# Attention block with a two-expert feed-forward: weighing the values with one 32-bit product per block instead of three 16-bit ones

## The reference, cut to what matters

```python
x = x + _L0_conv_ref(_ln_c(x), qkv_w, rpb, proj_w, proj_b)      # x: (8, 128, 56, 56)
t = _to_tokens(x)
t = t + _L0_ffn_ref(_ln_t(t), W_router, W1, b1, W2, b2)         # top 2 of 8 experts
x = _from_tokens(t, x)

def _L0_conv_ref(x, qkv_w, rpb, proj_w, proj_b):                # 16 heads of 8, window 7x7
    ...
    attn = jax.nn.softmax(logits, axis=-1)                      # over 49 neighbours
    for a in range(KSZ):
        va = jnp.take(v, si + a, axis=2)
        for c in range(KSZ):
            vac = jnp.take(va, sj + c, axis=3)
            out = out + attn[..., t, None] * vac
            t += 1
    y = out @ proj_w.T + proj_b
```

## Time and profile before

| | |
|---|---|
| time, 3 runs | 3146.11, 3155.05, 3156.77 us; median 3155.05 us |
| profiled execution | 3149.2 us, its span 3147.4 us |
| busy in the span | PE 79%, PEld 67%, DVE 75%, ACT 67%, POOL 75% |
| granted TensorE clock, mean | 0.904 |
| `scores` of the first and last unit | 84.5 us and 2264.7 us after the span's start |
| first and last product of the experts | 2366.4 us and 2965.3 us |

### The profile page before, as it was taken

How to read it: one execution, slowest core, us unless ns; L and a number is a source line. 1 busy time by engine, 2 the same in 40 slices (tenths; PEclk the granted TensorE clock), 3 DMA queues, 4 the chain that set the end, 5 groups by cost and what they waited for, 6 DMA issues and landing times. The chain is left out here.

```text
span 3147.4 us, 119476 instructions
## 1 busy us (share of the span) xinstructions
PE 2482.8 (79%) x34587; PEld 2108.7 (67%) x34692; DVE 2353.8 (75%) x12579; ACT 2122.5 (67%) x5724; POOL 2360.1 (75%) x2808
## 2 busy tenths in 40 slices
PE   4788887888788878888888878888709999999633
PEld 2677777777777777777777777777606666666522
DVE  2688887888788878888788878888746666666444
ACT  0677777777677777777777777777726777777400
POOL 2578888888888888888888888888946777777600
PEclk9999999999899999999999989999959999999855
DMA  2566555555555655555565555556455444444499
GB/s 49 145 126 119 121 124 119 114 122 118 112 106 122 123 118 110 118 117 117 114 120 118 118 109 119 121 117 123 92 99 94 93 92 93 93 93 92 98 314 299
DMA packets 743654, 378.47 MB, mean 120 GB/s; under 512 B 414595, under 2 KB 712227, under 8 KB 743078
## 3 DMA queue, kind: packets, MB, share of 16 engines
q1 hardware_dynamic: 690278, 235.46, 39.5%
q10 hardware_dynamic: 24192, 81.67, 9.9%
q0 software_dynamic: 28608, 54.48, 5.7%
HBM read 232.92 MB, written 98.11 MB: 105 GB/s over the span
## 5 line engine op out<-in xcount | busy, mean ns | idle before, releaser
L1004 ACT ACTIVATE pr<-sc,nmx 128x100 f32<-128x100 f32 x3136 | 922.3, 369 | 103.8 <-DVE nmx L670 100.6
L905 POOL TENSOR_TENSOR pl<-pt 100x512 f16<-100x512 f32 x784 | 815.3, 1040 | 217.9 <-ACT pt L1012 217.4
L670 DVE CUSTOM_DVE_ANT_0 sc<-bank,near 128x100 f32<-128x100 f32 x3136 | 632.3, 256 | 182.7 <-PE bank L490 133.4
L1012 ACT ACTIVATE pt<-bank 100x512 f32<-100x512 f32 x784 | 462.5, 590 | 365.9 <-PE bank L516 353.0
L490 PE MATMUL bank<-kimg,qexp 128*128 (+2 forms) x9408 | 651.5, 221 | 55.3 <-issue 40.0
L490 PEld LDWEIGHTS bank<-kimg,qexp 128*128 128x128 bf16 (+1 forms) x9408 | 567.7, 102 | 103.1 <-issue 71.7
L1385 POOL DMA_INDIRECT yrows<-ye,meta x420 | 451.1, 1074 | 188.6 <-issue 127.6
L516 PE MATMUL bank<-vwin,pt 100*128 100x65 bf16 (+1 forms) x6272 | 417.0, 199 | 202.7 <-DVE om L700 142.6
L516 PEld LDWEIGHTS bank<-vwin,pt 100*128 100x128 bf16 x6272 | 371.9, 102 | 277.1 <-issue 184.6
L911 POOL TENSOR_TENSOR oml<-om 128x256 f16<-128x256 f32 x784 | 483.4, 617 | 57.3 <-DVE om L700 35.4
L499 PE MATMUL bank<-cst_sb,pr 128*100 128x128 f32 x3136 | 503.9, 286 | 0.0
(11 more groups left out here) (150 smaller groups left out, 4665.4 us busy)
## 6 DMA issues: line engine op xcount, KB each, us to landing
vwin<-v_pix SPq DMA_DIRECT2D x1120, 60.5 KB
near<-bias_rows ACTq DMA_DIRECT2D x112, 600.0 KB
y<-yrows SPq DMA_DIRECT2D x112, 224.0 KB, 4.8
qexp<-qring SPq DMA_DIRECT2D x896, 14.0 KB
v_pix<-vrow SPq DMA_DIRECT2D x56, 225.8 KB
xin<-in_x SPq DMA_DIRECT2D x56, 224.0 KB
xres<-in_x SPq DMA_DIRECT2D x112, 112.0 KB, 4.6
x<-xres SPq DMA_DIRECT2D x112, 112.0 KB
```

The source lines that it names most:

```text
L670: i = v.tensor_tensor_reduce(out=sc[:, ring(m, par), k, :], in0=ps_s[m % 2][:, k, :], in1=near[:, st, ct, k, :], scale=-1.0, scalar=-MASKE ...
L905: g.tensor_tensor(pl[:, m % 2], pt[:, m % 2], pt_h[:, m % 2], ALU.subtract).then_inc(s["t_out"], 1)
L1004: i = a.activation(pr[:, r, k, :], sc[:, r, k, :], ACT.Exp, bias=nmx[:, r, k:k + 1], scale=-1.0)
L1012: i = a.activation(pt[:, m % 2].rearrange("p a q -> p (a q)"), ps_t[m % 2][0:NKEY, :], ACT.Copy)
```

## The change

The values are stored and loaded as one 32-bit number instead of two 16-bit halves of the same total size, ACT writes them from PSUM alone, and `a_v_l` on DVE is gone. The probabilities are used as they stand in `pt`; `split_t` on POOL and its tile `pl` are gone. `weigh` makes one 32-bit product per block and waits for the eviction (`th_done`). The lags of `weigh` and of all that follows it (`pick`, `split_l`, folding and projecting) become one slot shorter. The lag of the transposes stays.

```diff
-L_T, L_V, L_P, L_H, L_F = 3, 5, 6, 7, 8
+L_T, L_V, L_P, L_H, L_F = 3, 4, 5, 6, 7
...
-        vwin = asb("vwin", [NKEY, 2, NTILE, 2, VW], BF16)
+        vwin = asb("vwin", [NKEY, 2, NTILE, VW])
...
-                    pe.wait_ge(s["t_out"], n + 1)
+                    pe.wait_ge(s["th_done"], n + 1)
...
-                            p_h, p_l = pt_h[:, m % 2, 2 * t + blk, :], pl[:, m % 2, 2 * t + blk, :]
-                            v_h, v_l = (vwin[:, st, 2 * u + t, part, 64 * blk:64 * blk + 65].bitcast(dt)
-                                        for part, dt in enumerate((BF16, FP16)))
-                            for n, (a_, b_) in enumerate(((p_h, v_h), (p_h, v_l), (p_l, v_h))):
-                                mm = pe.matmul(ps_av[m % 2][:, 2 * t + blk, :], a_, b_, start=n == 0, stop=n == 2)
+                            mm = pe.matmul(ps_av[m % 2][:, 2 * t + blk, :], pt[:, m % 2, 2 * t + blk, :],
+                                           vwin[:, st, 2 * u + t, 64 * blk:64 * blk + 65], start=True, stop=True)
...
-                def a_v_l(I):
...
-                LATE_STEPS = {9: a_q_l, 10: a_k_l, 12: a_v_l}
+                LATE_STEPS = {9: a_q_l, 10: a_k_l}
...
-                def split_t(J, m, par):
-
-                    n = UPP * J + m
-                    g.wait_ge(s["th_done"], n + 1)
-                    g.tensor_tensor(pl[:, m % 2], pt[:, m % 2], pt_h[:, m % 2], ALU.subtract).then_inc(s["t_out"], 1)
...
-                        i = a.activation(vrow[:, :, 0, 65 * blk:65 * blk + 64],
+                        i = a.activation(vrow[:, :, 65 * blk:65 * blk + 64],
...
-                    i.then_inc(s["v_h"], 1)
+                    i.then_inc(s["v_out"], 1)
```

More of the change, by code:

```diff
@@ L103, in sem @@
             return ctx.enter_context(nc.semaphore(name))
-        v_pix = nc.dram_tensor("v_pix", (B * IMG, 2, VW), BF16, kind="Internal").ap()
+        v_pix = nc.dram_tensor("v_pix", (B * IMG, VW), FP32, kind="Internal").ap()
         bias_rows = nc.dram_tensor("bias_rows", (3, 128, 3 * 4 * NKEY), FP32, kind="Internal").ap()
@@ L159, in build @@
         pad = asb("pad", [HEADS, PADW, PADW])
-        vrow = asb("vrow", [HALF, NROW, 2, VW], BF16)
+        vrow = asb("vrow", [HALF, NROW, VW])
         sc = asb("sc", [128, RING, 4, NKEY])
@@ L164, in build @@
         pt = asb("pt", [NKEY, 2, 4, 128])
-        pl = asb("pl", [NKEY, 2, 4, 128], FP16)
         rec = asb("rec", [128, 4])
@@ L204, in build @@
         rowsb = rows[:].bitcast(BF16)
-        pt_h = pt[:].bitcast(BF16)[:, :, :, 1::2]
         om_h = om[:].bitcast(BF16)[:, :, :, :, 1::2]
@@ L218, in build @@
         names = """w_in w_scaled w1_in cst_in rpb_in pad_out gath_in turned win_in bias_done zeroed pad_zero
-            x_in mean_done xc_done sq_done v_h sub_done th_done oml_done
+            x_in mean_done xc_done sq_done sub_done th_done oml_done
             var_done ve_done root_done spread_done xn_done q_done q_h q_out k_done k_h k_out v_done v_out v_store q_exp0 q_exp1
-            v_in0 v_in1 s_done max_done exp_done t_done t_out av_done rec_done orec_done om_done
+            v_in0 v_in1 s_done max_done exp_done t_done av_done rec_done orec_done om_done
             o_done o_out proj_done proj_out bias_out near_in0 near_in1 xres_in0 xres_in1 x1_store0 x1_store1
@@ L312, in store_v @@
                     sp.wait_ge(s["v_out"], I + 1)
-                    dst = bass.AP(v_pix.tensor, I * (PAIR * 2 * VW), [[2 * VW, HALF], [HALF * 2 * VW, NROW], [1, 2 * VW]])
-                    sp.dma_start(dst, vrow[:].rearrange("p n a c -> p n (a c)")).then_inc(s["v_store"], 16)
+                    dst = bass.AP(v_pix.tensor, I * (PAIR * VW), [[VW, HALF], [HALF * VW, NROW], [1, VW]])
+                    sp.dma_start(dst, vrow[:]).then_inc(s["v_store"], 16)
                 def spread_q(J, par):
@@ L332, in windows @@
                         sp.wait_ge(s["av_done"], UPP * J - UPP + UNITS * (st + 1))
-                    at = ((J // NPAIR) * IMG + krow(J, st) * W) * (2 * VW)
+                    at = ((J // NPAIR) * IMG + krow(J, st) * W) * VW
                     for kr in range(KW):
-                        src = bass.AP(v_pix.tensor, at + (kr * W + 1) * (2 * VW), [[2 * VW, KW], [TS * 2 * VW, NTILE - 2], [1, 2 * VW]])
-                        sp.dma_start(vwin[kr * KW:(kr + 1) * KW, st, 1:NTILE - 1].rearrange("p t a c -> p t (a c)"), src).then_inc(s[f"v_in{st}"], 16)
+                        src = bass.AP(v_pix.tensor, at + (kr * W + 1) * VW, [[VW, KW], [TS * VW, NTILE - 2], [1, VW]])
+                        sp.dma_start(vwin[kr * KW:(kr + 1) * KW, st, 1:NTILE - 1], src).then_inc(s[f"v_in{st}"], 16)
                     for t, c0 in ((0, 0), (NTILE - 1, W - KW)):
-                        src = bass.AP(v_pix.tensor, at + c0 * (2 * VW), [[W * 2 * VW, KW], [2 * VW, KW], [1, 2 * VW]])
-                        sp.dma_start(vwin[:, st, t].rearrange("p a c -> p (a c)"), src).then_inc(s[f"v_in{st}"], 16)
+                        src = bass.AP(v_pix.tensor, at + c0 * VW, [[W * VW, KW], [VW, KW], [1, VW]])
+                        sp.dma_start(vwin[:, st, t], src).then_inc(s[f"v_in{st}"], 16)
                 def load_res(J, st):
@@ L604, in _ @@
                 v.memset(qexp[:, 1].rearrange("p s t h q -> p (s t h q)"), 0.0).then_inc(s["zeroed"], 1)
-                v.memset(vrow[:, :, 1, 64:65], 0.0)
-                v.memset(vrow[:, :, 0, 64:65], 1.0).then_inc(s["pad_zero"], 1)
+                v.memset(vrow[:, :, 64:65], 1.0).then_inc(s["pad_zero"], 1)
                 v.memset(ones_b[:], 1.0)
@@ L917, in body @@
                                 subtract(J, m, par)
-                            for d, step in ((L_H, split_l), (L_T, split_t)):
-                                if reached(J, m, d):
-                                    step(*back(J, m, par, d))
+                            if reached(J, m, L_H):
+                                split_l(*back(J, m, par, L_H))
                         if I is not None and m == A_ROOT:
@@ L931, in _ @@
                 for m in range(L_H):
-                    for d, step in ((L_H, split_l), (L_T, split_t)):
-                        if m < d:
-                            step(*back(PAIRS, m, PAIRS % 2, d))
+                    split_l(*back(PAIRS, m, PAIRS % 2, L_H))
                 for Q in range(PAIRS - 3, PAIRS):
```

## The result

The changed kernel is faster: 3083.4 us median (3075.7 to 3085.1, 4 runs) against 3155.9 (3146.1 to 3160.9, 4 runs), ratio 0.977, 95% interval 0.974 to 0.980. The forecast was 3265 us, slower. The time of rival A, 3082 us, is what was measured; the profiled execution took 3082.4 us, its span 3080.6.

The account below looks back on a forecast made before the run. No engine full; buffer hand-offs between engines set the 39.6 us pair. PE 29.6 + 8.1, loop turn 0.7, waits 1.5 make 39.9; clock 1.7 more gives 41.6, over 56 pairs 3265 us; range 3085 to 3450 (forecast's own 3190 to 3340).

Parts of the forecast that it names:

- rival A: Attention step: the clock holds and the waits go; 38.4 us a pair, 3082 us; chance 0.20.
- POOL's relief: POOL in the attention: without `split_t`, PE's waits for POOL, 2.1 us a pair, are gone.
- The `pick` waits remain in kind, because DVE keeps its long slot 11 (`gapr` alone 1.61 us): PE in slots 12 and 13: of 2.15 us waited behind DVE's slot 11, 1.0 stays.
- my 1.5 us a pair: PE's waits after the change: 1.0 us for `pick`, raised to 1.5 in all for slot 11 and the eviction.
- some tenths: DVE's slot 11 may begin some tenths later, behind ACT's eviction and key copy and DVE's key residue.
- The clock: PE after slot 13's wait: one half-clock stretch of 3.3 us a pair loses 1.7 us, giving 41.6.
- about as now: Sign in the attention: the mean clock stays about as now, 0.92 before the change.
- The price of the product: PE's new `weigh`: 0.95 us, 0.58 more per slot, 8.1 us a pair.
- my lower bound of 0.88: PE's new `weigh`: at least 0.88 us for eight loads, from transposes at 110 ns each.
- The lag: `weigh` one slot nearer to its scores: needs ACT's eviction, only moves ACT, not the bound; transfers costed at nothing.
- rival D: `weigh` would wait for ACT's eviction: 0.5 us a pair, 28 us more, inside the range; no separate chance given.
- Rival C: Attention: the clock stays low for long, 10 us a pair at 0.50; 44.9 us a pair, 3446 us; chance 0.23.

Follow-up runs that it names:

- experiment 4: Kernel before with one small router product, `gapr`, moved from DVE's slot 11 to POOL, `split_t` kept: 3099.2 us, ratio 0.984.
- experiment 1: Changed kernel plus one idle POOL subtraction per slot, of `split_t`'s size, nothing waiting for its result: 3309.5 us, ratio 1.049 to the kernel before.
- experiment 6: Changed kernel plus an idle POOL subtraction per slot that waits for ACT's eviction, so it falls where `split_t` fell: 3369.8 us, ratio 1.068 to the kernel before.
- experiment 7: Kernel before without `split_t`, low halves `pl` left zero, `weigh` waiting for ACT's eviction, three products and lags kept: 2956.1 us, ratio 0.937.
- experiment 2: Changed kernel plus one idle POOL power of 112x4 numbers per slot, about 1.04 us long: 3088.0 us, ratio 0.980 to the kernel before.

## Why the prediction was wrong, point by point

Four measured times follow one another, each with one thing changed: before 3153; without POOL's subtraction 2956, -197; the 32-bit product in place of three 16-bit ones, with its value rows, 3047, +91; the new lags 3083, +36.

- **POOL's relief: right in its waits, and far too small.** The 2.1 us a pair that PE waited for POOL are gone; if each wait was worth its length, that is 118 us of the 197. The rest I put down to DVE: in the kernel before, one held instruction moved away gave 54 us (experiment 4). How much of the 197 each would give by itself isn't settled, since a late PE also costs clock; that the hold-ups alone are worth 226 to 286 us in the changed kernel is shown by experiments 1 and 6.
- **The step that failed: "The `pick` waits remain in kind, because DVE keeps its long slot 11 (`gapr` alone 1.61 us)".** The duration was read from the earlier trace rows as what the operation costs. It was mostly a standstill: the operation takes 0.15 us, the rest was POOL's `split_t` and `split_l`. The row could have told it: 112x4 numbers in 1.61 us, and, in the same timeline (shown above), `idxf` from 64 columns in 0.22. So slot 11 became short by the very edit that I had costed on POOL alone, and of my 1.5 us a pair 0.6 came. These 0.6 stand where I had put "some tenths": DVE's key residue waits for ACT's copy, and `pick` stands behind it without a gap. With them came 0.2 for `qring`, a wait that my sum put at nothing without a reason, though the table had it before, with 0.7 us a pair. The two waits, the first after the change and the second before it:

```profile
DVE kimg L641 <- ACT kimg L943: 49.9, 45, 1.2
```
```profile
PE bank L458 <- DVE qring L639: 33.0, 45, 1.0
```

- **The clock followed from that.** Without the wait of slot 13 there is no half-clock stretch inside the loop; at the turns 61.4 / 2 / 45.9 = 0.7 us a pair are lost, not 1.7. (That the mean clock would be "about as now" didn't follow from my own sum: 3.3 of 41.6 us at half clock make a mean of 0.96, not 0.92; measured is 0.98.) In the middle of the loop PE is busy 39.12 of 40 us at clock 1.00. The rule that I set beside rival A, by the Trainium skill's "TensorE: Matmul & The Clock Gate", section "Why this matters for your kernels" (no long gaps between matmuls, and the clock stays high), held: the trace agrees.
- **The price of the product: mis-sized.** A `weigh` at full clock now (timeline of one slot of the changed kernel, against the earlier trace rows):

```profile
1204.04 0.60 PE L497 MATMUL bank<-cst_sb,pr 128*100 128x128 f32 x4
1204.48 1.00 PE L510 MATMUL bank<-vwin,pt 100*128 100x65 f32 x8
1205.32 0.48 PE L488 MATMUL bank<-kimg,qexp 128*128 x6
```

It takes 0.84 us to the next step, below my lower bound of 0.88: 0.47 more than before and not 0.58, 6.6 us a pair and not 8.1. The row of `a_spread` was the worse neighbour, the transposes the better one. By the Trainium skill's "TensorE: Matmul & The Clock Gate", section "LDWEIGHTS (loading the stationary operand)", the estimate had been 6.9 us a pair; the trace agrees within 0.3.

- **Summed up.** PE's work 29.6 + 6.6 = 36.2; PE idle 1750 - 1688.6 = 61 us, 1.3 a pair (0.6 `pick`, 0.2 `qring`, 0.5 the turn); clock 0.7: 38.2 us, as measured. From my 41.6 the price takes 1.5, the waits and the turn 0.9, the clock 1.0. Neither correction alone gives a faster kernel: with the waits and the clock right my sum is 39.7, with the price right 40.1, against 39.6 before. The price costs only 91 us of the 56 x 6.6 = 370: experiment 7's kernel leaves PE idle for 4.6 us a pair (1600 - 1396 us in 400 to 2000, 44.7 pairs) and the changed kernel with old lags for 1.1, so 3.5 us a pair, 196 us, fill what was idle. The rest of the difference isn't traced.
- **Rival A's time was met in part by luck.** Its 38.4 us a pair were 37.7 of work and 0.7 of waits; measured were 36.2 of work and 2.0 of waits and low clock. It was right that the clock holds inside the loop, but its price was 1.5 too high and its waits and clock 1.3 too low. It also left out the 12 us by which the first full pair becomes longer.
- **The lag: wrong at nothing.** It cost 36 us, by the fold and the projection, not by a `weigh` that waits for ACT (rival D), of which PE shows no wait.
- **Rival C** would have been the nearer one had DVE stayed held. With the hold-up put back (experiment 6) the step is 43.6 us, beyond my 41.6, and the clock is at half, in 400 to 2150 us, in 30 stretches of 12.2 us on average, before in 63 of 4.4: my one of 3.3 us a pair was too little. That 32-bit products as such make these stretches longer isn't shown: experiment 1 has the same products, and 13 of its 38 stretches last 3.4 us; and `gapr` is held for longer in experiment 6 than before (2.48 us on average against 1.80).

## What to carry to other kernels

Before a duration in a trace is carried over as the cost of an operation, hold it against its size: here a row of four columns that lasted 1.6 us was mostly a standstill, and its cause was what ended a few hundredths of a microsecond ahead of it on another engine. When work leaves one engine, look on the others for such rows; what they lose can be worth more than the waits that name the engine. And a step that is moved along costs too: try each part of a shift by itself, here the weighing without the fold.

## What the hardware showed that I had not expected

A VectorE instruction of 4 columns with two SBUF operands takes 0.15 us by itself and up to 2.8 us when POOL runs large subtractions one behind the other; in the rows above it ends 0.03 us behind the one that held it. The profile counts the standstill as busy time and shows no wait for it, so that VectorE looked like an engine with 33 us of work a pair when it had 30. Its products with an operand in PSUM aren't lengthened: in experiment 6 the two of `om` run beside POOL's `split_l`, from 1232.80 on, and take 0.49 us; one `om` takes 0.285 us on average in every run here, with POOL's subtraction or without. The same holds for `idxf`, which reads one SBUF operand: 0.22 us in every run.

The Trainium skill says in "SBUF — State Buffer", section "Who interferes with whom", that VectorE and GpSimd share a pair of SBUF ports, and that a VectorE instruction with two SBUF inputs (beside a GpSimd instruction that reads SBUF), or a copy or cast in one of the fast modes, stands still for the whole of a GpSimd instruction that has the ports first. The runs agree for subtractions of 512 and 256 columns a partition. They don't for POOL's power of four columns: it lasts 1.04 us, and a `gap` with both inputs in SBUF that starts 0.20 us behind its start takes 0.15. Here the measurement decides: how long POOL's instruction lasted did not count (experiment 2). Whether the amount of data or the kind of operation did, no run here separates.
